# A fused two-layer kernel: the setup's bias part, engine orders, copy issue and second-step split rearranged

## The reference, cut to what matters

```
# layer 0
h   = gelu(gelu(cond @ W0 + b0) @ W1 + b1)
att = softmax(h @ W2 + b2)                       # 128 x 8
agg_w = einsum('bk,koi->boi', att, weight)       # a 64 x 64 matrix for each batch entry
agg_b = att @ bias_k                             # 128 x 64
t   = einsum('boi,bih->boh', agg_w, x) + agg_b[:, :, None]
x   = x + t @ (A @ B.T).T + bias                 # rank 128
# layer 1
y   = conv1d(x, weight, 9 taps, pad 4, 4 groups) + (cond @ c_weight.T)[:, :, None] + fside[None, :, None]
top1 = argmax(y @ gate_w.T + expert_bias)        # 4 experts
x   = x + y @ W_up + lora_B[top1](lora_A[top1](y))
```

## Time and profile before

| | |
|---|---|
| median of three runs | 1211.03 us (1209.45 to 1213.23) |
| the profiled execution | 1210.87 us, of which the traced span is 1209.0 us |
| PE busy | 1165.1 us (96%) |
| PEld busy | 1061.5 us (88%) |
| DVE busy | 757.5 us (63%) |
| ACT busy | 435.5 us (36%) |

### The profile page before, as it was taken

How to read it: one execution, slowest core, us unless ns; L and a number is a source line. 1 busy time by engine, 2 the same in 40 slices (tenths; PEclk the granted TensorE clock), 3 DMA queues, 4 the chain that set the end, 5 groups by cost and what they waited for, 6 DMA issues and landing times.

```text
span 1209.0 us, 18805 instructions
## 1 busy us (share of the span) xinstructions
PE 1165.1 (96%) x7456; PEld 1061.5 (88%) x7456; DVE 757.5 (63%) x1512; ACT 435.5 (36%) x667; POOL 9.3 (1%) x22
## 2 busy tenths in 40 slices
PE   5668999999999999999999999999999999999998
PEld 4557999999999999999999999999999999999998
DVE  5736666666666666665666666566676566667652
ACT  4533332443333334333333433333343333334220
POOL 3000000000000000000000000000000000000000
PEclk9778999999999999999999999999999999999999
DMA  9533545444454544455454445445444554544211
GB/s 333 173 94 83 135 136 139 104 110 141 126 129 134 138 112 108 136 131 126 132 140 112 108 133 137 121 132 142 111 108 131 145 114 132 141 113 108 72 52 53
DMA packets 113866, 151.88 MB, mean 126 GB/s; under 512 B 21372, under 2 KB 91644, under 8 KB 109532
## 3 DMA queue, kind: packets, MB, share of 16 engines
q1 hardware_dynamic: 111876, 147.83, 45.6%
q10 hardware_dynamic: 1904, 2.86, 0.6%
HBM read 81.00 MB, written 35.68 MB: 97 GB/s over the span
## 4 chain that ended last, share of the span: by engine, by line
PE 93%; DVE 3%; DMA 2%; ACT 1%; SPq 1%; ACTq 1%; issue 0%; DVEq 0%
PE O L806 61%; PE F L791 8%; PE F L759 8%; PE F L779 4%; PE O L825 3%; PE F L729 2%; PE F L731 2%; PE F L730 2%; DMA Xr<-x 1%; SPq L220 1%; PE F L746 1%; DMA agb_scratch<-small 1%; PE F L747 1%; PE O L817 1%; DVE wks L610 0%; DVE xTl L480 0%
## 5 line engine op out<-in xcount | busy, mean ns | idle before, releaser
L806 PE MATMUL O<-Wh,yh 128*128 128x292 f32 (+2 forms) x1536 | 509.2, 331 | 0.0
L806 PE MATMUL O<-Wh,yl 128*128 128x292 f32 (+2 forms) x1536 | 497.6, 324 | 0.0
L806 PE MATMUL O<-Wl,yh 128*128 128x292 f32 (+2 forms) x1536 | 497.3, 324 | 0.0
L806 PEld LDWEIGHTS O<-Wh,yh 128*128 128x128 f32 x1536 | 289.4, 188 | 22.7
L806 PEld LDWEIGHTS O<-Wh,yl 128*128 128x128 f32 x1536 | 289.1, 188 | 22.9
L806 PEld LDWEIGHTS O<-Wl,yh 128*128 128x128 f32 x1536 | 289.9, 189 | 16.9
L580 DVE TENSOR_TENSOR osb<-O,x 128x256 f32<-128x256 f32 (+1 forms) x192 | 97.6, 508 | 107.4 <-PE O L825 107.4
L297 ACT ACTIVATE F<-F 128x512 f32<-128x512 f32 x126 | 73.3, 582 | 246.3 <-PE F L779 246.3
L537 DVE STREAM_TRANSPOSE yr<-F 128x512 f32<-128x512 f32 x128 | 91.1, 712 | 60.5 <-PE F L791 60.5
L297 ACT ACTIVATE u<-F 128x256 f32<-128x256 f32 x64 | 24.6, 384 | 275.2 <-PE F L731 230.4
L511 DVE TENSOR_TENSOR x<-F,x 128x512 f32<-128x512 f32 x128 | 88.0, 689 | 38.1 <-PE F L759 38.1
(11 more groups left out here) (136 smaller groups left out, 1529.4 us busy)
## 6 DMA issues: line engine op xcount, KB each, us to landing
x<-in_xP_dram SPq DMA_DIRECT2D x64, 516.0 KB, 4.5
xTr<-in_xT_dram SPq DMA_DIRECT2D x32, 1024.0 KB, 5.9
out_dram<-osb SPq DMA_DIRECT2D x64, 512.0 KB, 2.9
Xr<-x SPq DMA_DIRECT2D x504, 64.5 KB, 2.5
Wr<-in_Wd_dram SPq DMA_DIRECT2D x8, 530.0 KB, 13.5
agb<-agb_scratch SPq DMA_DIRECT2D x31, 128.0 KB, 3.2
agg_scratch<-stage ACTq DMA_DIRECT2D x1, 2048.0 KB, 10.8
agg<-agg_scratch SPq DMA_DIRECT2D x60, 32.0 KB, 2.5
```

The lines of the kernel that those rows point to most:

```text
L806: last = pe.matmul(O[c][:, 0:w_], w[:, t % YR, k, :], m[:, k, c0:c0 + w_], start=k == 0 and n_ == 0, stop=k == 7 and n_ == 2)
```

## The change

The changes are all in the setup, ahead of the loop, and in one wait of `load_agb`:

1. The first step's `agb` no longer goes out to memory and back. PE makes it by four products of 64 columns, each with one column of `atsT` spread over 128 as its weights; DVE copies it from PSUM. `agbs` is still made (now in bank `O[1]`) and written to `agb_scratch` for the later steps; SP now waits for that write ahead of its first read.
2. ACT evacuates six of the eight `agg_` banks (two on DVE), where it was four and four. ACT's order becomes: `Ah`, the four `bias(0)` copies, then the copies of `u`, with one split of W between, then `Th` and the other splits of W, the second step's x split (`txh(1)`) after `w(5)`.
3. On PE the conditioning products move ahead of `unit_u(0)`, and the second step's u, transpose and v products ahead of `wsum`.
4. DVE splits the second step's x (`txl(1)`) after `w(5)`, does the second step's `vv` and `vlo` between the first step's two `xd`, and `txl(2)` ahead of `ys(0, 1)`; ACT does `txh(2)` there too.
5. SP issues the eight transfers `rx(0, 1)` behind `rx(0, 0)`; ACT issued them before. `load_xT(2)` stands directly behind them.

The diff, with what the prediction doesn't speak of cut:

```diff
@@ SP @@
                 sp.wait_ge(v_v, s)
+                if s == 1:
+                    sp.wait_ge(d_abw, 16)
...
             load_agb(1)
             rx(0, 0)
+            rx(0, 1)
+            load_xT(2)
 
             sp.wait_ge(d_gw, 16)
             sp.wait_ge(d_gg, 128)
             load_x(2)
             load_x(3)
-            load_xT(2)
             load_agg(2)
@@ ACT @@
-            evac(0)
-            evac(2)
-            evac(4)
-            evac(6)
-            act.wait_ge(v_ag, 4)
-            act.wait_ge(a_ag, 4)
+            for c in (0, 2, 4, 5, 6, 7):
+                evac(c)
+            act.wait_ge(v_ag, 2)
+            act.wait_ge(a_ag, 6)
...
+            act.wait_ge(d_a, 16)
+            copy(Ah[:, :, :], Ar[:, :, :]).then_inc(a_a, 1)
+            bias(0)
+            ut(0)
             act.wait_ge(v_agb, 1)
             act.dma_start(agbD, agbs).then_inc(d_abw, 16)
-            act.wait_ge(d_a, 16)
-            copy(Ah[:, :, :], Ar[:, :, :]).then_inc(a_a, 1)
+            tuu(0)
             w(0)
-            act.wait_ge(d_abw, 16)
-            act.dma_start(agb[:, :], agbD[0:4, :].rearrange("(a b) o -> a (b o)", a=1).broadcast_to([128, 256])).then_inc(d_ag, 16)
+            vhi(0)
             act.dma_start(aggD.rearrange("n i o -> n (i o)"), stage[:, :]).then_inc(d_gw, 16)
             act.wait_ge(v_t, 1)
             copy(Th[:, :, :, :], Tr[:, :, :, :]).then_inc(a_t, 1)
-            w(1)
-            ut(0)
-            tuu(0)
-            bias(0)
-            w(2)
-            w(3)
-            vhi(0)
+            for k in range(1, 4):
+                w(k)
...
             act.wait_ge(p_cb, 2)
             act.wait_ge(d_abw, 16)
-            act.wait_ge(v_x1, 4)
-            for g in range(2):
-                for b in range(4):
-                    p0 = 64 * g + 16 * b
-                    act.dma_start(raw(0, 1)[:, 4 * g + b, :], x1[p0:p0 + 16, 1, :, :]).then_inc(d_rx[1], 16)
...
             pc(0, 3)
+            txh(2)
             ys(0, 1)
             bias(1)
-            txh(2)
             xs(1, 0)
@@ DVE @@
-            evac(5)
-            evac(7)
-            dve.wait_ge(p_agb, 1)
-            dve.tensor_copy(agbs, F[4][:, 256:320]).then_inc(v_agb, 1)
             txl(0, 0)
             txl(0, 1)
+            dve.wait_ge(p_agb, 2)
+            dve.tensor_copy(agbs, O[1][:, 0:64]).then_inc(v_agb, 1)
+            dve.tensor_copy(agb[:, :], F[4][:, 256:512]).then_inc(v_agb, 1)
...
@@ PE @@
-            pe.matmul(F[4][:, 256:320], atsT[:, :], wks[:, 4096:4160], start=True, stop=True).then_inc(p_agb, 1)
-
+
+            pe.wait_ge(v_ag, 1)
+            pe.matmul(O[1][:, 0:64], atsT[:, :], wks[:, 4096:4160], start=True, stop=True).then_inc(p_agb, 1)
+            for b in range(4):
+                last = pe.matmul(F[4][:, 256 + 64 * b:320 + 64 * b], atsT[:, b:b + 1].broadcast_to([24, 128]), wks[:, 4096:4160],
+                                 start=True, stop=True)
+            last.then_inc(p_agb, 1)
...
-            unit_u(0)
-            unit_tu(0)
             pe.wait_ge(g_cc, 5)
-            pe.wait_ge(v_cs, 1)
             for q in range(2):
...
                 last.then_inc(p_cb, 1)
+            unit_u(0)
+            unit_tu(0)
             unit_v(0)
             for i in range(4):
                 unit_o(0, i)
+            unit_u(1)
+            unit_tu(1)
+            unit_v(1)
             wsum(0)
             wsum(1)
             wsum(2)
-            unit_u(1)
-            unit_tu(1)
-            unit_v(1)
             pe.wait_ge(v_ws, 3)
```

More of the change, by code:

```diff
@@ L414, in _ @@
             copy(Th[:, :, :, :], Tr[:, :, :, :]).then_inc(a_t, 1)
-            w(1)
-            ut(0)
-            tuu(0)
-            bias(0)
-            w(2)
-            w(3)
-            vhi(0)
-            act.wait_ge(v_wk, 4)
-            for k in range(4, 8):
-                w(k)
+            for k in range(1, 4):
+                w(k)
+            act.wait_ge(v_wk, 4)
+            w(4)
+            w(5)
+            txh(1)
+            w(6)
+            w(7)
+            act.wait_ge(d_l, 16)
+            copy(Ls[0:96, :], Lr[:, :]).then_inc(a_l, 1)
             act.wait_ge(p_cb, 2)
             act.wait_ge(d_abw, 16)
-            act.wait_ge(v_x1, 4)
-            for g in range(2):
-                for b in range(4):
-                    p0 = 64 * g + 16 * b
-                    act.dma_start(raw(0, 1)[:, 4 * g + b, :], x1[p0:p0 + 16, 1, :, :]).then_inc(d_rx[1], 16)
-            act.wait_ge(d_l, 16)
-            copy(Ls[0:96, :], Lr[:, :]).then_inc(a_l, 1)
-            txh(1)
             xs(0, 0)
+            ut(1)
+            tuu(1)
+            vhi(1)
             act.wait_ge(v_l, 1)
@@ L485, in vv @@
                 dve.wait_ge(p_v, s + 1)
[L486 removed]
+                if s > 0:
+                    dve.wait_ge(d_ag, 16 * s)
                 if s == 0:
@@ L618, in _ @@
             evac(3)
[L619 to L622 removed]
             txl(0, 0)
             txl(0, 1)
+            dve.wait_ge(p_agb, 2)
+            dve.tensor_copy(agbs, O[1][:, 0:64]).then_inc(v_agb, 1)
+            dve.tensor_copy(agb[:, :], F[4][:, 256:512]).then_inc(v_agb, 1)
+            dve.wait_ge(d_t, 16)
+            dve.tensor_tensor(Tr[:, :, 2, :], Tr[:, :, 0, :], Tr[:, :, 1, :], ALU.add).then_inc(v_t, 1)
+            dve.wait_ge(d_fs, 16)
+            dve.wait_ge(p_cb, 2)
+            dve.tensor_copy(csB[:, :], O[2][:, 64:65]).then_inc(v_cs, 1)
+            for q in range(2):
+                dve.tensor_scalar(cbn[:, :, q], O[2][:, 32 * q:32 * q + 32], fsB[:, q:q + 1], None, ALU.add).then_inc(v_cb, 1)
             dve.wait_ge(a_a, 1)
             dve.tensor_tensor(Al[:, :, :], Ar[:, :, :], Ah[:, :, :].bitcast(fp32), ALU.subtract).then_inc(v_a, 1)
[L627 to L638 removed]
             cbf = cbn[:, :, :].rearrange("p s q -> p (s q)")
@@ L641, in _ @@
             dve.tensor_copy(cb3[:, :, 2].bitcast(f32r), cbf).then_inc(v_cb, 1)
+            w(0)
             vv(0)
-            w(2)
-            vlo(0)
-            w(3)
-            addx(0, 0)
-            addx(0, 1)
-            addx(0, 2)
-            addx(0, 3)
-            for k in range(4, 8):
-                w(k)
-            dve.wait_ge(a_l, 1)
-            dve.tensor_tensor(Ls[64:96, :], Lr[64:96, :], Ls[64:96, :].bitcast(fp32), ALU.subtract).then_inc(v_l, 1)
-            xd(0, 0)
-            xd(0, 1)
-            xs(0, 0)
-            xs(0, 1)
-            txl(1, 0)
-            txl(1, 1)
             dve.wait_ge(v_cb, 3)
@@ L662, in _ @@
             dve.tensor_scalar(cb3[:, :, 0].bitcast(f32r), cb3[:, :, 2], -1.0, None, ALU.mult).then_inc(v_cb, 1)
+            vlo(0)
+            dve.wait_ge(a_t, 1)
+            dve.tensor_tensor(Tl[:, :, :, :], Tr[:, :, :, :], Th[:, :, :, :].bitcast(fp32), ALU.subtract).then_inc(v_t, 1)
+            addx(0, 0)
+            addx(0, 1)
+            w(1)
+            addx(0, 2)
+            addx(0, 3)
+            w(2)
+            w(3)
+            w(4)
+            w(5)
+            txl(1, 0)
+            txl(1, 1)
+            w(6)
+            w(7)
+            xd(0, 0)
+            dve.wait_ge(a_l, 1)
+            dve.tensor_tensor(Ls[64:96, :], Lr[64:96, :], Ls[64:96, :].bitcast(fp32), ALU.subtract).then_inc(v_l, 1)
+            xs(0, 0)
+            vv(1)
+            vlo(1)
+            xd(0, 1)
+            xs(0, 1)
             dve.wait_ge(a_ws, 1)
@@ L676, in _ @@
             ty(0, 3)
+            txl(2, 0)
+            txl(2, 1)
             ys(0, 1)
@@ L680, in _ @@
             xd(1, 0)
-            txl(2, 0)
-            txl(2, 1)
             xs(1, 0)
@@ L862, in _ @@
                 pe.matmul(O[2][:, 64:66], Bh[:, c, :], onesr[:, 0:2], start=c == 0, stop=False)
-                last = pe.matmul(O[2][:, 64:66], Bl[:, c, :], onesr[:, 0:2], start=False, stop=c == 7)
-            last.then_inc(p_b, 1)
-            unit_u(0)
-            unit_tu(0)
+                pe.matmul(O[2][:, 64:66], Bl[:, c, :], onesr[:, 0:2], start=False, stop=c == 7)
             pe.wait_ge(g_cc, 5)
-            pe.wait_ge(v_cs, 1)
             for q in range(2):
```

27 lines of the change are left out of this document (6 added, 21 removed).

## The result

The changed kernel takes 1200.68 us, the median of four runs (1199.61 to 1202.11), beside 1210.88 us for the kernel before on the same chip (four runs, 1209.45 to 1213.23). The ratio is 0.9915, with a 95% interval from 0.9896 to 0.9934: 10.2 us faster. The forecast was 4.7 us faster, 1206.3. The profiled execution took 1200.43 us, of which the span is 1198.7, 10.3 less than before; the difference lies inside the span.

What follows compares the result with a forecast made beforehand. The loop is bound by PE, so only the start of `unit_zt(0)` counts: 6.6 us earlier, less 1.9 us lost to half clock behind it, gives -4.7 us and 1206.3 us; range 1203.0 to 1210.5.

Steps and rivals of the forecast that it cites:

- two nearly equal paths: Before the loop, PE's own work and the regrouping transfers both reach `unit_zt(0)` at 106.91; the 8.45 us wait lies beside.
- The queue edit's gain at nothing: Issuing `rx(0, 1)` on SP: landed by 52 to 54, needed at 57.1; ACT's freed 5.5 us gains only splits that weren't late.
- Spread weights: First step's bias part on PE: four products at 0.21 us each, between 0.5 and 2.3 us in all.
- Rival D: SP's list: `load_agb(1)` lands at 47.9, `rx(0, 0)` starts 9.5 us late; 1.6 us slower, 1212.6; chance 0.08.
- What takes most of it back: W's column sums now follow `unit_u(1)`: 7.8 us plus 1.6 for slow products, convolution from 65.2, only 4.6 us earlier.
- all terms of the clock: PE's half-pace stretches: 1.6 us added to W's sums, 1.4 gained in the convolution, 1.9 lost behind `unit_zt(0)`.
- DVE's run: DVE bounds from 35.9 us: `Tl`, four `addx`, five splits of W, two halves of `xTl`, until `unit_u(1)` at 48.5.
- The forecast's stretch: In W's column sums on PE, 3.4 us of the sums run at half pace, adding 1.6 us.
- the forecast shift: `unit_zt(0)`, PE's last wait of note ahead of the full loop, starts at 100.3 instead of 106.91, 6.6 us earlier.
- Rival B: W's column sums keep full clock, ending 1.6 us earlier; slow stretch at the end costs 1.3; 1204.1 us; chance 0.20.
- the restart: PE restarts at `unit_zt(0)` at half clock after 5.7 us idle: 1.9 us lost, bounds 1.3 and 2.9.
- C: Clock takes more: sums slow for 5 us, `unit_o(1)` and end at their worst; 2.3 us faster, 1208.7; chance 0.30.

Runs made afterwards that it cites:

- b_split3: Kernel before with only the third step's x split (`txh(2)`, `txl(2)`) moved ahead of `ys(0, 1)`: 1210.76 us, ratio 1.0002 to the kernel before.
- a_split3_late: Changed kernel with the third step's x split back behind `xd(1, 0)`: 1200.25 us, ratio 0.9920 to the kernel before.
- a_rx_act: Changed kernel with the eight transfers `rx(0, 1)` issued by ACT again, ahead of `xs(0, 0)`: 1202.46 us, ratio 0.9932 to the kernel before.
- a_look: Changed kernel, unchanged, profiled a second time: 1203.26 us, span 1201.5.
- a_warm: Changed kernel with products of unused result keeping PE busy in its setup and first-iteration waits: 1200.35 us, ratio 0.9919 to the kernel before.
- b_step1: Kernel before with the second step's u, transpose and v products ahead of W's column sums, DVE and ACT work moved accordingly: 1206.46 us, ratio 0.9963.
- b_look: Kernel before, unchanged, profiled a second time: 1211.1 us, span 1209.3.
- a_cond_late: Changed kernel with PE's conditioning products back behind `unit_tu(0)`: 1200.60 us, ratio 0.9916 to the kernel before.
- b_warm: Kernel before with products of unused result keeping PE busy in its waits; part of the result left out: 1206.99 us, ratio 0.9969.
- the filled kernels: `b_warm` and `a_warm`, the kernel before and the changed kernel with idle products in PE's waits: 1206.99 and 1200.35 us.

## Why the forecast was right in kind and wrong in size

**Right.** What bounds: the loop is PE's, two nearly equal paths lead to `unit_zt(0)`, and the longest wait lies beside the path (`b_split3`, `a_split3_late`). The chain between: `unit_u(0)` at 23.7 (23.68), `unit_u(1)` at 48.5 (46.53, 2.0 earlier), the wait at the third step's transpose 4.7 us (4.79), the shared `Xr` as what holds `zc(0)`. The queue edit's gain at nothing (`a_rx_act`, within the noise). Spread weights at 0.21 us a product: four in 1.04 us, and the next group starts 0.97 us behind their start. Rival D did not occur: `load_agb(1)` was issued at 33.52, 3.9 us later than the forecast's 29.6, and `rx(0, 0)` still at 37.17, right behind the second `addx`.

**The step that failed** is the one headed "What takes most of it back", and with it all terms of the clock. By its own steps, the 11.19 us of `unit_zt(0)` against the 6.6 forecast divide so:

| step | forecast | measured | gained over the forecast |
|---|---|---|---|
| `unit_u(0)` done, u copied | 29.1 | 28.28 | 0.8 |
| to `vv(0)` and to `Tl` | 33.0, 35.9 | 31.76, 34.19 | 0.9 |
| DVE's run to `unit_u(1)` | 12.6 | 12.34 | 0.3 |
| `unit_u(1)` to `vv(1)` | 7.3 | 7.23 | 0.1 |
| sums of W, to the convolution | 9.4 | 7.55 | 1.85 |
| convolution to `unit_o(1)` | 9.1 | 9.34 | -0.25 |
| to the second `addx` done | 3.65 | 3.0 | 0.65 |
| transfers to `xd(1, 0)` | 7.36 | 6.95 | 0.4 |
| `xd(1, 0)` to `unit_zt(0)` | 15.0 | 15.1 | -0.1 |

Together 4.6, and the loss behind `unit_zt(0)` was 0.9 us where 1.9 stood in the sum: 1.0 more. That is the 5.6 us between 1206.3 and 1200.7. Of it some 4 is the clock: 0.7 of the first row, 1.6 of the 1.85, 0.65 and 1.0. Two sums of the forecast are off by 0.1 (DVE's run adds up to 48.6, the sums of W at full clock to 7.7), which changes nothing. The sums of W were put down for 3.4 us at half clock, taken over from the convolution's slow products behind 69.81 in before, which stand in the same place, behind `unit_u(1)`'s transposes. What the runs showed in its place: in the eleven traces in which PE goes from `unit_v(1)` into the sums in after's order (after, `a_look`, `a_warm` and eight of the variants), they ran at full clock each time, 8.2 us from `vv(1)` to the first `pc`. In after the clock had risen at 50.9, within `unit_u(1)`, and held. `unit_u(0)` came to full pace 3.3 us after its start, where the forecast had before's 4.9, and `unit_o(1)` came to its first products at full clock and was slow only from 71.45 on, where before's was slow from its first.

The forecast's stretch exists, though: `b_step1` has it, with 9.39 us from `vv(1)` to the first `pc`, just the forecast's 9.4. And the slow products at 69.81 that it was taken from are there again in `b_look` and missing in `b_split3`. So one profile's slow stretch was carried over as if it belonged to the place. Why it comes in some runs and not in others is open. The idle time of PE ahead of it doesn't settle it: before the transposes it was 0.47 us in before, 1.68 in `b_step1`, and 1.22 in `a_cond_late`, whose sums were fast.

The same fault the other way round: the forecast hardly asked what before loses on its path. `b_warm` measures this, 4.0 us net, ahead of and in `unit_u(1)`, in the convolution and in `unit_o(1)`. Since the change moves the sums of W, 7.6 us of full work, between `unit_u(1)` and the convolution, PE comes to the convolution fast. The forecast had this effect at 1.4 us (1.17 measured) and set 1.6 us for the sums against it. That the filled kernels are 6.6 us apart and the forecast shift was 6.6 us is luck: the shift held clock terms of its own, and up to `unit_zt(0)` the filled kernels are only 5.7 us apart.

The other 1.6 us or so are hand-offs. The forecast's times leave room for ACT's issues of `agb_scratch` and `agg_scratch` in line with its copies; the rows show the issue of 0.35 us at the same start, 28.28, as the copy. Rival B, the sums at full clock, was nearest in kind (1204.1). It lacked the faster `unit_u(0)` and `unit_o(1)`, the hand-offs, and 0.4 us at the restart. Of C nothing came in after: no part of the sums was slow. Its long restart came in `a_look`, 2.4 us.
